# Self attention in steps of one sequence: near and far queries together on TensorE, scores over all 128 rows, one PSUM bank of values

## Chip, cores and metric

One NeuronCore of a Trainium2 chip runs the whole program. The metric is the device time of one execution in microseconds; a program's time is the median of its runs. Lower is better.

## What is computed

A decoder block on x of shape (32, 64, 512): self attention, cross attention to a context of the same shape, and a feed-forward part with routed experts, each with a residual sum. Only the self attention is touched. From the reference, cut down:

```python
q = (x @ wq).reshape(b, s, 32, 16)        # 32 heads of 16, s = 64
k = (x @ wk).reshape(b, s, 8, 16)         # 8 groups, each shared by 4 heads
v = (x @ wv).reshape(b, s, 8, 16)
scores = einsum('bihd,bjhd->bhij', q, repeat(k, 4)) * 16 ** -0.5
scores = where(tril(ones(s, s)), scores, finfo.min)
out = einsum('bhij,bjhd->bihd', softmax(scores), repeat(v, 4))
x = x + out.reshape(b, s, 512) @ wo
```

## The kernel before

The batch is worked in two halves of 16 sequences (8 tiles of 128 tokens, two sequences in each). Each half passes through projections, self attention, cross attention and the feed-forward part. Every engine has a program of its own, written out by hand, and semaphores tie them: a `wait_ge` holds back all that stands behind it on that engine.

`self_attention(half)` works in **units**. Unit u is sequence b = u // 2 with the query rows l = u % 2: the near half (l = 0, queries 0 to 31, which see 32 keys) or the far half (l = 1, queries 32 to 63, which see 64 keys). With 4 heads a group and 32 queries a unit's scores have 128 rows, and 8 groups times 32 or 64 keys as columns: 256 or 512. There are 32 units in a half.

- Keys are spread out for all groups at once: `spread_keys(b)` on DVE (line 1408) multiplies the sequence's transposed keys `kt` by a selector and writes `kbd` (in the space `kspace`), which has two buffers. Before, `gsel4` keeps 4 groups in 64 rows each, so `kbd` has 4 x 64 columns and the scores come from two matmuls of 64 rows.
- Scores: `scores1(u)` on PE writes two half banks (`pair`): two bf16 matmuls with an identity add the causal mask (line 615), two plain 32-bit matmuls over 64 rows each the scores (line 620). It waits for `kbd_done` and for the copy of the unit before.
- Softmax: `copy_scores` (ACT, 1028) takes the scores to `prob`, which has six buffers (`URING`); `unit_max` (DVE, 1417), `unit_subtract_max` (POOL, 1745), `unit_exps` (ACT, 900), `unit_sums` (DVE, a sum at 1422 and a reciprocal at 1425), `unit_normalise` (POOL, 1751).
- `transpose_probs` (PE, 473) transposes into the bank `pt`, `evacuate_probs` (ACT, 904) copies that to `probt`.
- `values1` (PE, 635) makes four matmuls over 32 columns of the array with `vbd`, the values as `spread_values` (ACT, 1022) lays them out. Four units fill one of two banks `ot`; `output_hi` (ACT, 907) and `output_lo` (DVE, 1301 through 1230) split it into two 32-bit parts.
- `project_part` (PE, 484 through 429 to 431) makes a quarter of the output projection of a tile, three matmuls; `updated` (DVE, 1429) adds it to x. Then follow the statistics of the second norm, `second_norm`, its transposition (PE, 447) and its split.
- Work from elsewhere fills the gaps: the self queries 5 to 7 (`self_query_part`, three matmuls each), and the splits of the weights for cross attention (`split_piece`: ACT 887, POOL 1720).

The engines' loops run over u, w and v, one unit at a time. PE computes the scores of unit u + 4 (`LEAD`), transposes u and takes the values of u - 1, then a part of a projection. On DVE the spreading of keys stands ahead of the maximum of the unit that is two ahead of its use:

```python
for w in range(UNITS1 + 4):                      # DVE
    if w % 2 == 0 and 2 <= w // 2 + 1 < NSEQ:
        spread_keys(w // 2 + 1)
    if w < UNITS1:
        unit_max(w)
    if 1 <= w <= UNITS1:
        unit_sums(w - 1)
```

## Time and profile before

| | |
|---|---|
| median of 3 runs | 1687.55 us (1687.44 to 1689.91) |
| the profiled execution | 1689.26 us, span of its profile 1687.5 us |
| busy over the span: PE | 1621.2 us, 96% |
| PE weight loads | 1328.7 us, 79% |
| DVE | 1111.7 us, 66% |
| ACT | 750.4 us, 44% |
| POOL | 622.8 us, 37% |
| the chain that ended last, by engine | PE 88%, DVE 6%, ACT 2%, issue 2% |

PE is TensorE, DVE VectorE, ACT ScalarE, POOL GpSimd. Busy time is the time in which at least one instruction of the engine ran. The chain is followed back from the last instruction, at each step to what released it. Two stretches of the span hold the self attention: about 65 to 160 us for the first half and 898 to 993 us for the second. A plain 32-bit matmul leaves two records, one of a 32-bit transposition one, and records of neighbours overlap, since each counts a pipeline's latency; what an instruction takes in a stream is the distance from start to start.

### The profile page before, as it was taken

Reading aid. Unit: us, or ns where it says so; the run is one execution under the profiler, and the core shown is the slowest. Engines: PE = TensorE matmul, PEld = TensorE weight load, DVE = VectorE, ACT = ScalarE, POOL = GpSimd, SP = SyncE. Lnnn points to the kernel's source line nnn. Section 1 sums busy time; section 2 is a strip of 40 time slices with the busy share of each in tenths; the row PEclk is TensorE's granted clock in tenths of the full one; section 3 lists DMA queues with packets and bytes.
Section 4 is the critical chain, followed back from the end, with each engine's and each line's share of the span. In section 5 each row is a group of like instructions: output and inputs, shape, how many; then the busy total and the mean of one; then the engine's idle time right before and its main releaser. Section 6 shows DMA issues by size and latency. Waiting matters only on the chain.

```text
span 1687.5 us, 41365 instructions
## 1 busy us (share of the span) xinstructions
PE 1621.2 (96%) x17048; PEld 1328.7 (79%) x17048; DVE 1111.7 (66%) x1979; ACT 750.4 (44%) x1396; POOL 622.8 (37%) x515
## 2 busy tenths in 40 slices
PE   5899999999999999999988999999999999998998
PEld 5556788888888888788865578888888888886897
DVE  4477767676766676874544868676676767668643
ACT  2585535354454444431225745455353544443221
POOL 3484423334243332460125834243233342434500
PEclk9999999999999999999999999999999999998999
DMA  4210112021020120121121102021020110201100
GB/s 167 63 45 1 26 40 63 0 62 44 19 62 8 54 68 0 51 82 47 46 61 61 32 1 64 2 63 37 25 62 0 62 44 19 68 18 46 39 20 26
DMA packets 26254, 71.59 MB, mean 42 GB/s; under 512 B 3136, under 2 KB 3392, under 8 KB 26176
## 3 DMA queue, kind: packets, MB, share of 16 engines
q1 hardware_dynamic: 26176, 70.48, 13.5%
q8 instruction: 57, 0.93, 0.2%
q14 instruction: 21, 0.17, 0.0%
HBM read 66.27 MB, written 4.19 MB: 42 GB/s over the span
## 4 chain that ended last, share of the span: by engine, by line
PE 88%; DVE 6%; ACT 2%; issue 2%; POOL 1%; DMA 1%; POOLq 0%; SPq 0%; DVEq 0%; ACTq 0%
PE acc L429 15%; PE acc L430 14%; PE acc L431 13%; PE y L429 10%; PE y L431 9%; PE y L430 9%; PE quad L707 5%; PE quad L736 4%; PE y L720 2%; PE y L473 2%; PE quad L620 2%; PE quad L635 1%; DVE kv L1391 1%; PE acc L447 1%; DVE qb L1395 1%
## 5 line engine op out<-in xcount | busy, mean ns | idle before, releaser
L1724 POOL TENSOR_TENSOR qkrs<-qkve,mhalf 128x10 f32<-128x10 f32 x64 | 125.1, 1954 | 328.9 <-DVE qkve L1383 328.9
L429 PE MATMUL y<-w_hi 128*128 128x512 f32 x576 | 233.6, 405 | 10.8 <-DVE w_lo L1230 9.7
L429 PE MATMUL acc<-w_hi,xn_hi 128*128 128x512 f32 (+1 forms) x576 | 228.0, 396 | 10.5 <-DVE xn_lo L1230 10.5
L430 PE MATMUL y<-w_lo,w_hi 128*128 128x512 f32 x576 | 226.5, 393 | 0.0
L431 PE MATMUL y<-w_hi,w_lo 128*128 128x512 f32 x576 | 226.2, 393 | 0.0
L430 PE MATMUL acc<-w_lo,xn_hi 128*128 128x512 f32 (+1 forms) x576 | 221.6, 385 | 0.0
L431 PE MATMUL acc<-w_hi,xn_lo 128*128 128x512 f32 (+1 forms) x576 | 219.8, 382 | 0.0
L1720 POOL TENSOR_TENSOR w_lo<-stage,w_hi 128x1024 fp32r<-128x1024 f32 (+1 forms) x88 | 171.6, 1958 | 86.1 <-ACT w_hi L887 86.1
L1306 DVE TENSOR_TENSOR x<-y,x 128x512 f32<-128x512 f32 x128 | 88.4, 691 | 146.5 <-PE y L431 146.5
L1377 DVE TENSOR_REDUCE qkss<-kspace 128x4 f32<-128x512 f32 x128 | 87.4, 683 | 110.9 <-ACT kspace L926 110.2
L429 PE MATMUL acc<-w_hi,cx_hi 128*128 128x256 f32 x512 | 151.1, 295 | 1.7 <-DVE xn_lo L1230 1.7
L429 PEld LDWEIGHTS acc<-w_hi,xn_hi 128*128 128x128 f32 x576 | 110.7, 192 | 50.6 <-issue 23.9
L430 PE MATMUL acc<-w_lo,cx_hi 128*128 128x256 f32 x512 | 145.8, 285 | 0.0
L431 PE MATMUL acc<-w_hi,cx_lo 128*128 128x256 f32 x512 | 145.8, 285 | 0.0
L1733 POOL TENSOR_TENSOR prob<-prob,pmax 128x512 f32<-128x512 f32 x64 | 69.3, 1082 | 206.6 <-DVE pmax L1289 206.6
L429 PEld LDWEIGHTS y<-w_hi 128*128 128x128 f32 x576 | 109.1, 189 | 43.3 <-issue 22.8
L1101 ACT COPY probt<-y 128x512 f32<-128x512 f32 x64 | 37.6, 588 | 234.5 <-PE y L720 234.5
L887 ACT CAST w_hi<-stage 128x1024 fp32r<-128x1024 f32 (+1 forms) x116 | 104.8, 918 | 82.0 <-PE y L431 63.9
L431 PEld LDWEIGHTS acc<-w_hi,xn_lo 128*128 128x128 f32 x576 | 110.8, 192 | 21.6
L431 PEld LDWEIGHTS y<-w_hi,w_lo 128*128 128x128 f32 x576 | 109.3, 190 | 23.5
L430 PEld LDWEIGHTS y<-w_lo,w_hi 128*128 128x128 f32 x576 | 109.4, 190 | 20.2
L430 PEld LDWEIGHTS acc<-w_lo,xn_hi 128*128 128x128 f32 x576 | 110.9, 193 | 18.0
(139 smaller groups left out, 3737.4 us busy)
## 6 DMA issues: line engine op xcount, KB each, us to landing
stage<-in_w_cross SPq DMA_DIRECT2D x64, 512.0 KB, 3.7
stage<-in_w_cross SPq DMA_DIRECT2D x32, 256.0 KB, 2.8
stage<-in_w_ffn SPq DMA_DIRECT2D x16, 512.0 KB, 3.6
x<-in_x SPq DMA_DIRECT2D x8, 512.0 KB, 4.0
stage<-in_w_self SPq DMA_DIRECT2D x8, 512.0 KB, 4.8
kt<-in_ctx SPq DMA_DIRECT2D x16, 256.0 KB, 3.0
out_x<-x SPq DMA_DIRECT2D x16, 256.0 KB, 2.0
stage<-in_w_self SPq DMA_DIRECT2D x4, 256.0 KB, 4.5
```

The source lines that it names most:

```text
L429: nc.tensor.matmul(target, l_hi, r_hi, start=first, stop=False)
L430: nc.tensor.matmul(target, l_hi, r_lo, start=False, stop=False)
L431: return nc.tensor.matmul(target, l_lo, r_hi, start=False, stop=last)
L707: ins = nc.tensor.matmul(quad[h * SEQ:(h + 1) * SEQ, i, t * SEQ:(t + 1) * SEQ], q2t[rows, t, j, 2 * h:2 * h + 2, :].rearrange("p h q -> p ...
L736: ins = nc.tensor.matmul(ot[:, b, t * 256:(t + 1) * 256], kv[rows, 2 * (k % CHUNKS) + t, P:2 * P], probs, start=True, stop=True)
L887: nc.scalar.copy(target, stage[:, place.slot(n), 0:width]).then_inc(w_hi_done, 1)
L1101: nc.scalar.copy(probt[:, k % 2, :], y[0][:]).then_inc(pt_done.sem, 1)
L1306: nc.vector.tensor_tensor(x[:, i % NT, :], y[i % 2][:], x[:, i % NT, :], ALU.add).then_inc(y_free.sem, 1)
L1377: nc.vector.tensor_reduce(qkss[:, k % 2, t * REP:(t + 1) * REP], qsq[:, t], AX_X, ALU.add).then_inc(q_sum.sem, 1)
L1720: nc.gpsimd.tensor_tensor(low, stage[:, place.slot(n), 0:width], high.bitcast(F32), ALU.subtract).then_inc(w_lo_done, 1)
L1724: return nc.gpsimd.tensor_tensor(target, source, mhalf[:, 0:width], ALU.pow)
L1733: nc.gpsimd.tensor_tensor(pr, pr, spread(pmax[:, buffer, :], 8, SEQ), ALU.subtract).then_inc(s_sub.sem, 1)
```

## The change

Every loop of the self attention now goes over p, one sequence a step, with both its units. In a step p PE makes the scores of sequence p + 2 (`AHEAD`), the values of both units of p - 1, the transpositions of both units of p, and two parts of a projection.

- `kbd` has 8 groups x 64 keys (512 columns), each group's keys in its own 16 of 128 rows, so the scores of a unit are one matmul over 128 rows. The near unit's has 256 columns, the far one's 512. The mask comes behind them, one matmul of 256 columns each, the far one's over the far 32 keys alone. Each unit's scores have a bank (`sc[0]`, `sc[1]`).
- `gsel4` and its making go; `causal_b` has 8 x 32 columns.
- Transpositions alternate between two banks (`pt`), one of which was a bank of values; the values have one bank, `ot1`, so the first values of a tile wait for `output_lo` of the tile before.
- On DVE `spread_keys(p + 3)` stands behind the maxima and sums of the step and behind `output_lo`.

```diff
-                    pe.wait_ge(s_add.sem, at(s_add, u))
-                    keys = slice(0, SEQ) if l else slice(0, SEQ // 2)
-                    masks = slice(0, SEQ) if l else slice(SEQ // 2, SEQ)
-                    for t in range(2):
-                        nc.tensor.matmul(pair[:, t, :, keys], ident_b[:], causal_b[:, :, masks],
-                                         start=True, stop=False)
-
-                    for t in range(2):
-                        rows = slice(t * SEQ, (t + 1) * SEQ)
-                        ins = nc.tensor.matmul(pair[:, t, :, keys], q1t[rows, b, l].rearrange("p r q -> p (r q)"),
-                                               kbd[rows, b % 2, :, keys], start=False, stop=True)
-                    ins.then_inc(sc_rdy.sem, 1)
+                    near, far = (slice(l * SEQ // 2, (l + 1) * SEQ // 2) for l in range(2))
+                    queries = [q1t[:, b, l].rearrange("p r q -> p (r q)") for l in range(2)]
+
+                    pe.wait_ge(s_add.sem, at(s_add, max(2 * b - 1, 0)))
+                    nc.tensor.matmul(sc[0], queries[0], kbd[:, b % 2, :, near], start=True, stop=False)
+                    pe.wait_ge(s_add.sem, at(s_add, 2 * b))
+                    nc.tensor.matmul(sc[1], queries[1], kbd[:, b % 2], start=True, stop=False)
+                    nc.tensor.matmul(sc[0], ident_b[:], causal_b[:], start=False, stop=True).then_inc(sc_rdy.sem, 1)
+                    nc.tensor.matmul(sc[1][:, :, far], ident_b[:], causal_b[:], start=False, stop=True
+                                     ).then_inc(sc_rdy.sem, 1)
...
                     if u % 4 == 0:
-                        pe.wait_ge(ot_lo_done.sem, at(ot_lo_done, i - 1))
+                        pe.wait_ge(ot_lo_done.sem, at(ot_lo_done, i))
...
+                for p in range(NSEQ + 1):
+                    if p + AHEAD < NSEQ:
+                        scores1(p + AHEAD)
+                    if p == 0:
+                        query_parts(0)
+                    if p >= 1:
+                        values1(2 * p - 2)
+                        values1(2 * p - 1)
+                    if p < NSEQ:
+                        transpose_probs(at, 2 * p, (2 * p) % URING)
+                        transpose_probs(at, 2 * p + 1, (2 * p + 1) % URING)
+                    if 0 < p < 4:
+                        query_parts(p)
+                    if p == 4:
                         pieces_split(place, 5)
-                    if u >= 8:
-
-                        i = (u - 8) // 4
-                        project_part(at, i, i + 1, u % 4, self_y(i), i)
-                    if u >= 16 and u % 4 == 0:
-                        second_norm((u - 16) // 4)
-                for h in range(1, REP):
+                    if p >= 4:
+
+                        i = (p - 4) // 2
+                        for h in (2 * (p % 2), 2 * (p % 2) + 1):
+                            project_part(at, i, i + 1, h, self_y(i), i)
+                    if p >= 8 and p % 2 == 0:
+                        second_norm((p - 8) // 2)
+                for h in (2, 3):
                     project_part(at, 6, 7, h, self_y(6), 6)
...
+                for p in range(-AHEAD, NSEQ + 1):
+                    scored = p + AHEAD < NSEQ
+                    if p == -1:
                         self_queries(half, 5)
...
+                    if scored:
+                        copy_scores(2 * (p + AHEAD))
+                    if 0 <= p + 1 < NSEQ:
+                        unit_exps(at, 2 * (p + 1) + 1)
+                    if scored:
+                        copy_scores(2 * (p + AHEAD) + 1)
+                        unit_exps(at, 2 * (p + AHEAD))
...
+                for p in range(-AHEAD, NSEQ + 1):
+                    scored = p + AHEAD < NSEQ
+                    if p >= 6 and p % 2 == 0:
+                        updated((p - 6) // 2)
+                    if p >= 9 and p % 2 == 1:
+                        second_norm_lo((p - 9) // 2)
+                    if scored:
+                        unit_max(2 * (p + AHEAD))
+                    if 0 <= p + 1 < NSEQ:
+                        unit_sums(2 * (p + 1) + 1)
+                    if scored:
+                        unit_max(2 * (p + AHEAD) + 1)
+                        unit_sums(2 * (p + AHEAD))
+                    if p >= 2 and p % 2 == 0:
+                        output_lo(at, (p - 2) // 2)
+                    if 2 <= p + 3 < NSEQ:
+                        spread_keys(p + 3)
...
+                for p in range(-AHEAD, NSEQ):
+                    scored = p + AHEAD < NSEQ
+                    if scored:
+                        unit_subtract_max(at, 2 * (p + AHEAD))
+                    if p >= 7 and p % 2 == 1:
+                        layernorm_rstd(at, NT, (p - 7) // 2)
+                    if 0 <= p + 1 < NSEQ:
+                        unit_normalise(at, 2 * (p + 1) + 1)
+                    if scored:
+                        unit_subtract_max(at, 2 * (p + AHEAD) + 1)
+                        unit_normalise(at, 2 * (p + AHEAD))
```

The last three loops are those of ACT, DVE and POOL; the order of PE's and DVE's instructions decides most, and so it is shown twice.

First PE, in the steady part of the stage, before the change: one sequence, that is two units. `quad<-causal_b` is the mask, `quad<-kspace,qb` the scores, `y1<-ident,prob` the transpositions, `quad<-probt,vbd` the values.

```order
L615 MATMUL quad<-causal_b,ident_b 128x4x32 [waits s_add,kbd_done]
L615 MATMUL quad<-causal_b,ident_b 128x4x32
L620 MATMUL quad<-kspace,qb 128x4x32 x2
L473 MATMUL y1<-ident,prob 128x128 [waits pt_done,s_nrm]
L473 MATMUL y1<-ident,prob 128x128 x3
L635 MATMUL quad<-probt,vbd 32x4x32 [waits vbd_done,pt_done]
L635 MATMUL quad<-probt,vbd 32x4x32 x3
L429 MATMUL acc1<-xn_hi,w_hi 128x512
L430 MATMUL acc1<-xn_lo,w_hi 128x512
L431 MATMUL acc1<-xn_hi,w_lo 128x512
L615 MATMUL quad<-causal_b,ident_b 128x256 [waits s_add,kbd_done]
L615 MATMUL quad<-causal_b,ident_b 128x256
```

And PE after the change, one step:

```order
L616 MATMUL quad<-kspace,qb 128x256 [waits s_add,kbd_done]
L618 MATMUL quad<-kspace,qb 128x512 [waits s_add]
L619 MATMUL quad<-causal_b,ident_b 128x256
L620 MATMUL quad<-causal_b,ident_b 128x8x32
L634 MATMUL quad<-probt,vbd 32x4x32 [waits vbd_done,pt_done]
L634 MATMUL quad<-probt,vbd 32x4x32 x3
L634 MATMUL quad<-probt,vbd 32x4x32 [waits vbd_done,pt_done]
L634 MATMUL quad<-probt,vbd 32x4x32 x3
L475 MATMUL quad<-ident,prob 128x128 [waits pt_done,s_nrm]
L475 MATMUL quad<-ident,prob 128x128 x3
L475 MATMUL y1<-ident,prob 128x128 [waits pt_done,s_nrm]
L475 MATMUL y1<-ident,prob 128x128 x3
```

The same kinds of matmul stand together, and `kbd_done` is waited for once a sequence, ahead of everything else of the step.

Then DVE, before: two units and the keys of the sequence after. `kspace<-kt,gsel4` is `spread_keys`.

```order
L1408 TENSOR_TENSOR kspace<-kt,gsel4 128x256 [waits sc_rdy]
L1417 TENSOR_REDUCE pmax<-prob 128x8 [waits s_add]
L1422 TENSOR_REDUCE psum_<-prob 128x8 [waits s_exp]
L1425 RECIPROCAL prec<-psum_ 128x8 [waits s_sum]
L1417 TENSOR_REDUCE pmax<-prob 128x8 [waits s_add]
L1422 TENSOR_REDUCE psum_<-prob 128x8 [waits s_exp]
L1425 RECIPROCAL prec<-psum_ 128x8 [waits s_sum]
L1230 TENSOR_TENSOR w_lo<-quad,w_hi 128x2x4x64 [waits ot_hi_done]
L1408 TENSOR_TENSOR kspace<-kt,gsel4 128x256 [waits sc_rdy]
```

And DVE after the change, one step with an `output_lo`:

```order
L1418 TENSOR_REDUCE pmax<-prob 128x8 [waits s_add]
L1423 TENSOR_REDUCE psum_<-prob 128x8 [waits s_exp]
L1426 RECIPROCAL prec<-psum_ 128x8 [waits s_sum]
L1418 TENSOR_REDUCE pmax<-prob 128x8 [waits s_add]
L1423 TENSOR_REDUCE psum_<-prob 128x8 [waits s_exp]
L1426 RECIPROCAL prec<-psum_ 128x8 [waits s_sum]
L1234 TENSOR_TENSOR w_lo<-quad,w_hi 128x2x4x64 [waits ot_hi_done]
L1409 TENSOR_TENSOR kspace<-kt,gsel 128x512 [waits sc_rdy]
```

The four reductions that now stand ahead of `kspace` are the near maximum of sequence p + 2, the far sum of p + 1, the far maximum and the near sum of p + 2; `kspace` is for p + 3. So the keys of sequence b stand behind all of the reductions of the near unit of b - 1; before, they stood ahead of the first one.

## Rows read from the trace of the kernel before

**Rows 1.** Windows: us; busy us of PE, PEld, DVE, ACT, POOL; PE clock, DMA, GB/s
```profile
100.00:130.00 30.00, 30.00 (x252) 17.93 (x251) 25.18 (x58) 23.12 (x52) 26.26 (x29) 1.00 0.15 46
890.00:910.00 20.00, 16.11 (x86) 11.13 (x85) 7.46 (x18) 8.89 (x20) 6.77 (x8) 0.91 0.19 67
```

**Rows 2.** Waits, 64 to 160 us: engine line <- releaser: total us, times, longest us
```profile
PEld quad L615 <- DVE kspace L1408: 0.6, 2, 0.3
```

**Rows 3.** Timeline, PE, one sequence: start, us, what; later [idle before <-releaser]
```profile
101.55 0.29 PE L615 MATMUL quad<-causal_b,ident_b 128*128 128x128 bf16 x2
101.76 0.49 PE L620 MATMUL quad<-kspace,qb 64*128 64x128 f32 x4
102.19 0.66 PE L473 MATMUL y<-ident,prob 128*128 128x128 f32 x4
102.77 0.43 PE L635 MATMUL quad<-probt,vbd 128*32 128x128 f32 x8
...
103.95 0.40 PE L615 MATMUL quad<-causal_b,ident_b 128*128 128x256 bf16 x2
104.27 0.70 PE L620 MATMUL quad<-kspace,qb 64*128 64x256 f32 x4
104.91 0.66 PE L473 MATMUL y<-ident,prob 128*128 128x128 f32 x4
...
106.67 0.29 PE L615 MATMUL quad<-causal_b,ident_b 128*128 128x128 bf16 x2
```

**Rows 4.** Chain of waits: plain 32-bit matmuls, 128 rows, 512 columns (two records each)
```profile
60.48 3.44 PE y L497 x8
```

**Rows 5.** Timeline, PE: scores of sequence 0, 2, 15; first matmul after the stage
```profile
68.17 0.28 PE L615 MATMUL quad<-causal_b,ident_b 128*128 128x128 bf16 x2
...
76.19 0.27 PE L615 MATMUL quad<-causal_b,ident_b 128*128 128x128 bf16 x2 [0.78 <-ACT prob L1028]
...
143.62 0.28 PE L615 MATMUL quad<-causal_b,ident_b 128*128 128x128 bf16 x2
...
160.35 0.28 PE L429 MATMUL acc<-w_hi,cx_hi 128*128 128x256 f32 x1
```

**Rows 6.** Timeline, ACT: copy of near scores, then the exponential of far ones
```profile
92.49 0.37 ACT L1028 COPY prob<-quad 128x256 f32<-128x256 f32 x1 [0.52 <-PE quad L620]
92.76 0.63 ACT L900 ACTIVATE prob<-prob 128x512 f32<-128x512 f32 x1
```

**Rows 7.** Timeline, DVE, the stage of the first half
```profile
85.88 0.69 DVE L1417 TENSOR_REDUCE pmax<-prob 128x8 f32<-128x512 f32 x1 [1.74 <-ACT prob L1028]
86.48 0.41 DVE L1422 TENSOR_REDUCE psum_<-prob 128x8 f32<-128x256 f32 x1
86.93 0.20 DVE L1425 RECIPROCAL prec<-psum_ 128x8 f32<-128x8 f32 x1
87.05 0.92 DVE L1408 TENSOR_TENSOR kspace<-kt,gsel 128x256 f32<-128x256 f32 x1
...
92.00 0.69 DVE L1230 TENSOR_TENSOR w_lo<-quad,w_hi 128x512 fp32r<-128x512 f32 x1
...
93.32 0.41 DVE L1417 TENSOR_REDUCE pmax<-prob 128x8 f32<-128x256 f32 x1
93.65 0.67 DVE L1422 TENSOR_REDUCE psum_<-prob 128x8 f32<-128x512 f32 x1
94.35 0.20 DVE L1425 RECIPROCAL prec<-psum_ 128x8 f32<-128x8 f32 x1
```

**Rows 8.** Timeline, POOL, the same stage
```profile
86.65 1.04 POOL L1745 TENSOR_TENSOR prob<-prob,pmax 128x512 f32<-128x512 f32 x1 [1.39 <-DVE pmax L1417]
...
94.64 1.04 POOL L1751 TENSOR_TENSOR prob<-prob,prec 128x512 f32<-128x512 f32 x1 [0.21 <-DVE prec L1425]
```

**Rows 9.** Timeline, POOL and DVE, two instructions that meet
```profile
77.22 1.31 POOL L1745 TENSOR_TENSOR prob<-prob,pmax 128x512 f32<-128x512 f32 x1
...
77.25 0.37 DVE L1408 TENSOR_TENSOR kspace<-kt,gsel 128x256 f32<-128x256 f32 x1
```

More of the change, by code:

```diff
@@ L39 @@
 ACC3 = NT + 7 * CHUNKS
-LEAD = 4
+AHEAD = 2
 PRING = 4
@@ L641, in self_attention @@
                 scores1(0)
-                self_query_part(half, 5, 0)
-                self_query_part(half, 5, 1)
+                self_queries(half, 5)
                 scores1(1)
-                self_query_part(half, 5, 2)
-                self_query_part(half, 5, 3)
-                scores1(2)
-                self_query_part(half, 6, 0)
-                scores1(3)
                 def second_norm(i):
@@ L1026, in copy_scores @@
                     act.wait_ge(sc_rdy.sem, at(sc_rdy, u + 1))
-                    target = seen(u, u % URING).rearrange("p (t g) k -> p t g k", t=2)
-                    nc.scalar.copy(target, pair[:, :, :, 0:target.shape[-1]]).then_inc(s_add.sem, 1)
+                    nc.scalar.copy(seen(u, u % URING), sc[u % 2]).then_inc(s_add.sem, 1)
                 spread_values(0)
@@ L1042, in second_norm_hi @@
                     transposed_hi(n_at, n, tile_of(xn_hi, i), ln_hi_done)
-                for w in range(UNITS1 + 4):
-                    if w < UNITS1:
-                        copy_scores(w)
-                    if w == 1:
+                for p in range(-AHEAD, NSEQ + 1):
+                    scored = p + AHEAD < NSEQ
+                    if p == -1:
                         self_queries(half, 5)
-                    if 1 <= w <= UNITS1:
-                        unit_exps(at, w - 1)
-                    if LEAD <= w < UNITS1 + LEAD:
-                        evacuate_probs(at, w - LEAD, (w - LEAD) % 2)
-                    if w in (6, 10):
-                        self_queries(half, w // 4 + 5)
-                    if w >= 9 and w % 4 == 1:
-                        i = (w - 9) // 4
+                    if scored:
[6 more added lines that the diff above has]
+                    if p >= 2 and p % 2 == 0:
+                        i = (p - 2) // 2
@@ L1068, in self_attention @@
+                    if p in (1, 3):
+                        self_queries(half, 6 + p // 2)
+                    if p >= 8 and p % 2 == 0:
+                        second_norm_hi((p - 8) // 2)
+                    if 0 <= p < NSEQ - 2:
+                        spread_values(p + 2)
+                    if p in (2, 4, 6, 8):
+                        act.wait_ge(acc_rdy.sem, at(acc_rdy, A1[half]["q7" if p > 4 else "kv3"] + 1))
+                        split_piece(Place(2, half, 0), (p - 2) // 2)
                 first = Place(2, half, 0)
-                act.wait_ge(pv_done.sem, at(pv_done, UNITS1))
@@ L1811, in self_attention @@
                                  0.0).then_inc(gaps_clear.sem, 1)
-                for v in range(UNITS1 + 1):
-                    if v < UNITS1:
-                        unit_subtract_max(at, v)
-                    if v >= 1:
-                        unit_normalise(at, v - 1)
-                    if v in (7, 11, 15, 19):
-                        split_piece(Place(2, half, 0), (v - 7) // 4)
-                    if v >= 17 and v % 4 == 1:
-                        layernorm_rstd(at, NT, (v - 17) // 4)
-                for i in (4, 5, 6):
+                for p in range(-AHEAD, NSEQ):
+                    scored = p + AHEAD < NSEQ
+                    if scored:
+                        unit_subtract_max(at, 2 * (p + AHEAD))
+                    if p >= 7 and p % 2 == 1:
+                        layernorm_rstd(at, NT, (p - 7) // 2)
[4 more added lines that the diff above has]
+                        unit_normalise(at, 2 * (p + AHEAD))
+                    if p in (2, 4, 6, 8):
+                        split_piece(Place(2, half, 0), (p - 2) // 2)
+                for i in (5, 6):
                     layernorm_rstd(at, NT, i)
```

90 lines of the change are left out of this document (30 added, 60 removed).

## The prediction

> **What bounds the kernel now.** I looked first at the windows, for who is busy in the stage that changes. In its steady part TensorE (PE) is busy for all of the 30 us, POOL for 26.26, DVE for 25.18, and PE's clock is granted in full [rows 1]. So PE sets the pace there, but DVE and POOL have under a sixth of slack, and less than that once an order forces them to wait. Then the waits: in the whole stage of the first half PE waited for the spread keys for 0.6 us, twice, 0.3 us at the longest [rows 2]. Third PE's timeline, for what a sequence costs: from the near unit's mask to that of the next sequence 5.12 us (101.55 to 106.67) [rows 3]. Last the timelines of ACT, DVE and POOL, for the distances from start to start from which a chain can be laid [rows 6 to 8]. I take faster or slower by over 0.2%, 3.4 us, as what a measurement can tell.
>
> **PE's own work.** Before, a sequence's masks and scores take 0.21 + 0.43 for the near unit and 0.32 + 0.64 for the far one, 1.60 us [rows 3]. The 64-row matmul with twice the columns takes only 0.21 more. A plain 32-bit matmul of 512 columns over 128 rows leaves 8 records in 3.44 us for four matmuls, 0.86 each [rows 4], so 128 columns are 0.21: two matmuls of 64 rows therefore run side by side, and the rest of 0.43 and of 0.64, 0.21 both times, is the change from one kind of matmul to the next. After, the near scores take 0.43, the far 0.86, the masks (2 x 256 columns, at 0.11 for the 2 x 128 of before, the part of 0.21 that is no change) 0.21, with a change or two of 0.1 between: 1.6 to 1.7. The scores gain nothing: three changes of kind are saved, and the side-by-side running is lost.
> The Trainium skill has a rule that speaks against this part ("TensorEngine Tiling (Array Packing)", Performance Considerations): a contraction of 64 rows can be packed in two tiles for up to twice the rate, while its Key Properties say that a change of tiling mode drains the engine. By the first alone the scores would cost 0.64 more a sequence; the rows have both.
> The values with a projection part take 1.18 a unit (102.77 to 103.95) and a unit's transpositions 0.58 (102.19 to 102.77) [rows 3]. In pairs I take 2.1 and 1.1, since each change of kind comes once instead of twice (0.1 to 0.15 each, by what is over in the row above). PE's step is then 1.65 + 2.1 + 1.1 = 4.85 against 5.12, a gain of 0.27, if nothing is late: 32 sequences, 8.6 us, at most.
>
> **What is late: the keys.** `scores1(p + 3)` waits for `spread_keys(p + 3)`, and DVE now comes to that only behind the near sum of sequence p + 2, which needs that sequence's scores. So each step closes a loop: scores, softmax of the near unit, keys, scores. I lay it out from the start of a step's scores, S = 0.
> - PE: the near mask, the third matmul, starts at 0.43 + 0.86 + 0.1 = 1.38 and its record is over 0.29 later, at 1.67 (that length is the 0.29 of the two small masks, taken long) [rows 3]. I give ACT 0.05 to see it, by estimate.
> - ACT: copy of the near scores at 1.72, 0.37 long, to 2.09. The far exponential of the sequence before stands behind it and starts 0.27 after its start, at 1.99, to 2.62 [rows 6].
> - DVE: near maximum from about 2.12, 0.41 long; then the far sum, which waits for that exponential: 2.65. From its start to its reciprocal 0.70, at 3.35 (93.65 to 94.35) [rows 7]; next instruction 0.12 later (86.93 to 87.05), the far maximum at 3.47; the near sum 0.60 after it (85.88 to 86.48), 4.07; its reciprocal 0.45 later, 4.52; and 0.12 later, at 4.64, `spread_keys`, or in every second step `output_lo` (0.69, of which 0.09 overlaps), with `spread_keys` at 5.25.
> - The spreading has 512 columns instead of 256. With nothing beside it 256 take 0.37 [rows 9]; 256 more add 0.28, as 0.69 against 0.41 of the reductions shows [rows 7]: 0.65.
> - It meets POOL. In the row at 87.05 it took 0.92: POOL's instruction from 86.65 ended at 87.69 [rows 8], and 0.28 later the keys were done, 87.97. So the two exclude each other, for a whole instruction, and a caught spreading ends 0.28 + 0.28 after POOL's. Here POOL's far normalising starts 0.09 after the far reciprocal's end (94.55 to 94.64) [rows 7, 8], at 3.64, to 4.68; the far subtraction follows at once, to 5.72.
> - Steps without `output_lo`: DVE asks at 4.64, gets its turn at 4.68, is done at 5.24. With PE's start, 0.15 by estimate, the next scores begin at S = 5.4. Steps with it: DVE asks at 5.25, in the far subtraction, waits until 5.72, is done at 6.28; S = 6.4.
> Both are longer than PE's 4.85, so PE waits 0.5 and 1.5 us a step. ACT has 3 copies and 2 exponentials of 0.4 to 0.6 a step besides the copies of probabilities, and ends before its next copy; the norms' work on DVE (about 1.7 in a step) fits into the 2.1 us in which it waits for scores. Those cost nothing. The single bank of values doesn't either: `output_lo` is over ahead of the keys, so ahead of the next scores.
>
> **The sum.** Scores of sequence 0 start at 68.17 as before [rows 5]. Then 1.65, and self query 5 in one piece, 2.8 by estimate (12 matmuls at the 0.23 or so that is left of 1.18 with the values taken out): the scores of sequence 1 at 72.6. Fourteen intervals follow to sequence 15, of which six have an `output_lo`: 8 x 5.4 + 6 x 6.4 = 81.6, so 154.2 in place of 143.62 [rows 5]: 10.6 late. Behind it nothing closes the loop. Before, 16.7 us were left to the first matmul after the stage (160.35); after, the scores (1.65), four pairs of values (2.4) and three of transpositions (3.3), five pairs of projection parts (7.2) and two norm transpositions (0.9, by estimate as the transpositions) come to 15.5, and 0.4 for a wait for `x`: 15.9, 0.8 less. That is 9.8 us a half, 20 in both. The first interval has PE idle for about 3.8 us, and once a stretch with shorter gaps lowered the granted clock to 0.91 on a mean of 20 us [rows 1], which is 3 to 4 us at 1.2 GHz, half the columns a us: I add 1 us a half. Sum: +22 on the profiled execution's 1689.26 us, 1711.3. The median of the runs is 1.7 lower, so I say **1710 us**, against 1687.55.
>
> **Rivals.**
> - *POOL wins each meeting* (0.22). DVE's 4.64 and POOL's 4.68 are close enough to go either way. If the far subtraction gets in first, the steps without `output_lo` are 6.4 too: 8 us more a half, 1726. For it: 0.1 us more on DVE does it. Against: where POOL's record started 0.03 ahead of DVE's, at 77.22, it was POOL that was drawn out, to 1.31 from 1.04, and the keys took their bare 0.37 [rows 9]. The Trainium skill ("SBUF — State Buffer", SBUF: two separate sides) says that whichever of the two starts first keeps the port pair for the whole instruction; by its letter POOL would have it there and often here, which is this rival. The row has the lock, but not by the recorded starts. Between the two lie mixed cases, and the weights' splits (POOL, four steps a half) shift the meeting.
> - *The keys are hardly late* (0.13). If the far sum were ready earlier or hand-overs were shorter, the loop would lose up to 0.4 a step: 5.1 and 6.0, so 5 us a half less, 1700.
> - *It is faster* (0.06). The mechanism: the loop fits beside PE's other work of a step, which is the 3.2 us between two scores. It decides where the near unit's softmax and the spreading take under 3.2 us from the end of the scores; I have 3.75 and 4.75. Then PE's saved changes of kind are paid out: 0.27 a sequence at best, 1680 to 1684. For it only that the 0.6 us of [rows 2] show keys ready before they are wanted, but in the old order.
> - *PE's clock falls throughout* (0.05). With 10 to 20% of idle time in each step the granted clock could drop again and again, as in the second window of [rows 1], where PE was busy for 16.1 of 20 us. At 0.9 over twice 90 us that is some 10 us of PE time more, partly inside the loop: 1720 or more.
>
> **How the numbers follow.** The forecast case has 0.52, with 1704 to 1717 as its own range (0.1 us on each hand-over of the loop makes 3 us in both halves). With the first two rivals it makes 0.87. The range 1698 to 1727 reaches just past both. Slower 0.92, the sum of all cases but one; faster 0.06; the same 0.02, for a loop that is just about as long as PE's step. That the change doesn't do what it says is no case: the order of both engines shows it.
>
> **What would show it.** Right: scores of a sequence 5.3 to 6.5 us apart, shorter and longer in turn; PE's greatest new wait before the scores, for DVE's `kspace`, some 13 to 17 us a half, all of it in that place; `kspace` at 128x512 taking 0.6 to 1.1 us; masks and scores about 1.65 us; sequence 15 near 154. Wrong: no wait for `kspace`; a PE step under 5 us; a wait for values or transpositions in its place; a granted clock well under 1 over the stage.

## The result, and the profile after

| | before | after |
|---|---|---|
| median | 1687.49 us (1686.67 to 1689.91, 4 runs) | 1710.62 us (1707.66 to 1712.84, 4 runs) |
| span of the profiled execution | 1687.5 us | 1709.1 us |
| scores of sequence 0 to the first matmul behind the stage, first half | 92.18 us | 103.11 us |
| the same, second half | 92.18 us | 103.11 us |

The ratio is 1.0128, with a 95% interval of 1.0111 to 1.0146: slower by 23 us. Both halves' stages are 10.93 us longer, 21.9 together, and the spans differ by 21.6: all of the loss lies in the stage that was changed.

The page of after, its first and fourth part (busy time by engine; the chain that ended last):

```profile
PE 1615.4 (95%) x16856; PEld 1337.8 (78%) x16856; DVE 1117.2 (65%) x1977; ACT 750.3 (44%) x1396; POOL 632.6 (37%) x515
...
PE 84%; DVE 10%; ACT 3%; issue 2%; POOL 1%; DMA 1%; POOLq 0%; SPq 0%; DVEq 0%; ACTq 0%
```

PE has 5.8 us less to do than before and the program is 22 us longer. The chain tells why: DVE's share of it rose from 6 to 10%, ACT's from 2 to 3%, and PE's fell from 88 to 84%.

Windows of after, columns as in [rows 1]: the second row is the one that answers to the first of [rows 1], and the first is discussed further down.

```profile
78.90:85.70 6.80, 6.75 (x21) 4.40 (x21) 2.95 (x7) 2.27 (x5) 3.72 (x5) 0.58 0.00 1
100.00:130.00 30.00, 24.79 (x189) 16.55 (x188) 21.02 (x46) 20.31 (x48) 23.19 (x24) 1.00 0.17 53
```

PE is busy for 24.79 of 30 us where it was for 30.00, and each of DVE, ACT and POOL does less in the window too. No engine is full, so what to look for is a loop through several engines.

Waits of after, 64 to 172 us, columns as in [rows 2]:

```profile
DVE pmax L1418 <- ACT prob L1030: 27.1, 16, 4.9
ACT prob L1030 <- PE quad L619: 26.9, 16, 4.8
...
PE quad L616 <- DVE kspace L1409: 16.4, 13, 3.5
```

Read from below, this is the loop: PE's scores wait for DVE's keys (16.4 us, where PE's only wait for them before was that of its weight loads in [rows 2], 0.6), ACT's copies for PE's scores, DVE's maxima for ACT's copies. Then PE's timeline, the starts of the scores of sequences 2 to 5, with most of step 2 from 90.95 on:

```profile
78.91 1.22 PE L616 MATMUL quad<-kspace,qb 128*128 128x256 f32 x2 [3.51 <-DVE kspace L1409]
...
85.67 0.70 PE L616 MATMUL quad<-kspace,qb 128*128 128x256 f32 x2
...
90.95 0.70 PE L616 MATMUL quad<-kspace,qb 128*128 128x256 f32 x2 [0.52 <-DVE kspace L1409]
91.49 1.02 PE L618 MATMUL quad<-kspace,qb 128*128 128x512 f32 x2
92.35 0.27 PE L619 MATMUL quad<-causal_b,ident_b 128*128 128x256 bf16 x1
...
92.66 0.64 PE L634 MATMUL quad<-probt,vbd 128*32 128x128 f32 x16
93.24 0.66 PE L475 MATMUL quad<-ident,prob 128*128 128x128 f32 x4
93.73 0.60 PE L475 MATMUL y<-ident,prob 128*128 128x128 f32 x4
94.08 0.48 PE L429 MATMUL acc<-xn_hi,w_hi 128*128 128x512 f32 x1
...
97.37 0.70 PE L616 MATMUL quad<-kspace,qb 128*128 128x256 f32 x2 [1.65 <-DVE kspace L1409]
```

Scores start 5.28 us apart (85.67 to 90.95) and then 6.42 (to 97.37); the next ones come 5.29 later, at 102.66, and 6.42 after that. Now DVE's timeline of a step with `output_lo`, and the end of the next one without; its scores begin at 90.95 and 97.37.

```profile
93.06 0.42 DVE L1418 TENSOR_REDUCE pmax<-prob 128x8 f32<-128x256 f32 x1 [2.16 <-ACT prob L1030]
...
95.68 0.64 DVE L1234 TENSOR_TENSOR w_lo<-quad,w_hi 128x512 fp32r<-128x512 f32 x1
96.23 1.08 DVE L1409 TENSOR_TENSOR kspace<-kt,gsel 128x512 f32<-128x512 f32 x1
...
101.97 0.64 DVE L1409 TENSOR_TENSOR kspace<-kt,gsel 128x512 f32<-128x512 f32 x1
```

And the POOL instructions that these two spreadings meet:

```profile
95.73 1.04 POOL L1748 TENSOR_TENSOR prob<-prob,pmax 128x512 f32<-128x512 f32 x1
...
102.02 1.49 POOL L1748 TENSOR_TENSOR prob<-prob,pmax 128x512 f32<-128x512 f32 x1
```

In the long step the far subtraction was under way, until 96.77; the keys were done 0.54 later, at 97.31, and PE started 0.06 after that. In the short step DVE asked at 4.60 us from the scores' start, 0.05 ahead of POOL: the keys took their bare 0.64, and POOL's instruction was drawn out to 1.49.

### The profile page after: what moved, and what is told of

Same layout as the page of the kernel before. It is cut to its first block, busy times and chain, and to the rows that moved or that the text cites. A ratio compares the mean times of both kernels' runs of the same rounds, so it can differ in the third digit from the quotient of the medians.

```text
span 1709.1 us, 40947 instructions
## 1 busy us (share of the span) xinstructions
PE 1615.4 (95%) x16856; PEld 1337.8 (78%) x16856; DVE 1117.2 (65%) x1977; ACT 750.3 (44%) x1396; POOL 632.6 (37%) x515
## 3 DMA queue, kind: packets, MB, share of 16 engines
HBM read 66.27 MB, written 4.19 MB: 41 GB/s over the span
## 4 chain that ended last, share of the span: by engine, by line
PE 84%; DVE 10%; ACT 3%; issue 2%; POOL 1%; DMA 1%; POOLq 0%; SPq 0%; DVEq 0%; ACTq 0%
PE acc L429 14%; PE acc L430 13%; PE acc L431 13%; PE y L429 9%; PE y L431 9%; PE y L430 9%; PE quad L710 5%; PE quad L739 4%; PE y L723 2%; PE quad L618 2%; DVE psum_ L1423 1%; PE quad L616 1%; DVE kspace L1409 1%; DVE kv L1393 1%; PE acc L447 1%
## 5 line engine op out<-in xcount | busy, mean ns | idle before, releaser
L890 ACT CAST w_hi<-stage 128x1024 fp32r<-128x1024 f32 (+1 forms) x116 | 104.8, 917 | 81.6 <-PE y L431 64.0
L431 PEld LDWEIGHTS acc<-w_hi,xn_lo 128*128 128x128 f32 x576 | 111.6, 194 | 21.6
```

The lines of the kernel that those rows point to most:

```text
L431: return nc.tensor.matmul(target, l_lo, r_hi, start=False, stop=last)
L890: nc.scalar.copy(target, stage[:, place.slot(n), 0:width]).then_inc(w_hi_done, 1)
```

## The experiments

Three questions were open. Is it the place of the keys behind the near sum, and nothing else, that costs the time? How much of it is POOL? And what would the rest of the change be worth with the keys in time? All ratios are to the kernel before, run beside each. That kernel's median was 1689.17 us beside the first four experiments, 1688.16 beside the next four and 1688.71 beside the last two, against 1687.49 beside the change, so a difference of microseconds between experiments of different groups is known to 1 or 2 us only.

### Keys first in the step

```diff
@@ DVE
                 for p in range(-AHEAD, NSEQ + 1):
                     scored = p + AHEAD < NSEQ
+                    if 2 <= p + 3 < NSEQ:
+                        spread_keys(p + 3)
...
                         output_lo(at, (p - 2) // 2)
-                    if 2 <= p + 3 < NSEQ:
-                        spread_keys(p + 3)
```

> The change with the spreading of keys moved to the head of DVE's step; nothing else. Theory (the keys close a loop behind the near unit's softmax): the wait of TensorE for the spread keys goes, the scores of a sequence start every 4.6 to 4.9 us, set by TensorE's own work of a step (4.6 us from one score to the end of the projection parts in the profile after), and the time falls below the kernel before, 1670 to 1682 us. Rival (the change costs by its wider matmuls and one bank of values, the wait for keys only hides that): TensorE waits in another place instead, for values or transpositions, and the time stays at 1700 us or more.

Measured: 1682.77 us (1680.22 to 1683.5), ratio 0.9958 (0.9942 to 0.9975). That is 28 us under after, by moving two lines, and just above what I expected. PE has no wait for the keys; of its waits for other engines in the first half's stage, 6.0 us in all against 2.3 in the kernel before, the two greatest are:

```profile
PE y L429 <- DVE x L1430: 3.0, 5, 1.1
PE quad L634 <- ACT probt L907: 1.3, 2, 0.7
```

One step of PE's timeline shows what the change itself does to PE, where nothing is late (from 95.08, behind a step of the same kinds):

```profile
95.08 0.59 PE L616 MATMUL quad<-kspace,qb 128*128 128x256 f32 x2
95.50 1.02 PE L618 MATMUL quad<-kspace,qb 128*128 128x512 f32 x2
96.36 0.27 PE L619 MATMUL quad<-causal_b,ident_b 128*128 128x256 bf16 x1
96.47 0.27 PE L620 MATMUL quad<-causal_b,ident_b 128*128 128x256 bf16 x1
96.67 0.64 PE L634 MATMUL quad<-probt,vbd 128*32 128x128 f32 x16
...
99.58 0.59 PE L616 MATMUL quad<-kspace,qb 128*128 128x256 f32 x2
```

The step is 4.50 long, against 5.12 in [rows 3]: 0.62 a sequence, 20 us for 32. Only 6 arrive. The steps on both sides of this one are 4.87 and 4.92 long, since the values wait for `vbd` (0.30 and 0.35 us, ACT's spreading of the values). Two steps of the half are much longer, 7.20 (114.00 to 121.20) and 7.25 (125.71 to 132.96). POOL, DVE and PE in the first of them:

```profile
112.35 2.39 POOL L1723 TENSOR_TENSOR w_lo<-stage,w_hi 128x1024 fp32r<-128x1024 f32 x1 [0.60 <-ACT w_hi L890]
...
115.79 0.42 DVE L1423 TENSOR_REDUCE psum_<-prob 128x8 f32<-128x256 f32 x1 [1.20 <-ACT prob L903]
...
117.03 1.53 DVE L1409 TENSOR_TENSOR kspace<-kt,gsel 128x512 f32<-128x512 f32 x1
...
119.31 0.47 PE L429 MATMUL y<-w_hi 128*128 128x512 f32 x1 [1.08 <-DVE x L1430]
```

POOL's split of a weight, 2.39 us, holds back the near subtraction, behind it the near exponential and `probt` (PE waits 0.62 us for that at 116.28), and the near sum, for which DVE stands idle 1.20 us. Then the keys take 1.53 us beside POOL's far subtraction, and `updated` (`x`) stands behind them. In this late part of the stage, where `updated` and the second norm's work are added, DVE has no slack to catch up:

```profile
130.00:145.00 15.00, 13.69 (x108) 9.60 (x108) 14.64 (x36) 11.42 (x29) 11.60 (x14) 1.00 0.01 2
```

A full DVE is still not the pace of each step: within this window one step takes 4.51 (132.96 to 137.47). `kspace` takes 1.00 us on the mean in this run against 0.87 in after, both in the first half's stage: here more of it falls on POOL's instructions.

### Keys ahead of `output_lo`

```diff
+                    if 2 <= p + 3 < NSEQ:
+                        spread_keys(p + 3)
                     if p >= 2 and p % 2 == 0:
                         output_lo(at, (p - 2) // 2)
-                    if 2 <= p + 3 < NSEQ:
-                        spread_keys(p + 3)
```

> The spreading one place earlier, ahead of output_lo and behind the near sum. Theory: the six longer intervals of a half (6.4 us) become as short as the others (5.3), 13 us less than the change in both halves, 1697 us. Rival (the long intervals come from other work that falls into each second step, the update of x or the weights' splits): no change, 1710 us.

Measured: 1702.89 us (1700.88 to 1703.68), ratio 1.0078 (1.0062 to 1.0095), 7.7 under after. In the early part the long interval is gone:

```profile
84.84 0.70 PE L616 MATMUL quad<-kspace,qb 128*128 128x256 f32 x2 [1.26 <-DVE kspace L1409]
90.13 0.70 PE L616 MATMUL quad<-kspace,qb 128*128 128x256 f32 x2 [0.53 <-DVE kspace L1409]
95.55 0.70 PE L616 MATMUL quad<-kspace,qb 128*128 128x256 f32 x2 [0.65 <-DVE kspace L1409]
```

They are 5.29 and 5.42 apart, and so on. So the 6.42 of every second step in after is `output_lo` and the POOL instruction that its delay runs into. Later two steps go wrong again, 6.45 us (117.14 to 123.59) and 7.04 (129.01 to 136.05). The step behind the second, 6.89, is another matter: its granted clock is 0.66 from 135 to 140 us, and the same step of the second half takes 5.42. DVE and POOL ahead of the first of the two:

```profile
118.52 2.37 POOL L1723 TENSOR_TENSOR w_lo<-stage,w_hi 128x1024 fp32r<-128x1024 f32 x1
...
120.86 0.61 POOL L1748 TENSOR_TENSOR prob<-prob,pmax 128x256 f32<-128x256 f32 x1
...
121.95 0.42 DVE L1423 TENSOR_REDUCE psum_<-prob 128x8 f32<-128x256 f32 x1 [0.70 <-ACT prob L903]
...
122.52 1.01 DVE L1409 TENSOR_TENSOR kspace<-kt,gsel 128x512 f32<-128x512 f32 x1
```

POOL's split of a weight, 2.37 us, holds back the near subtraction, with it the exponential, the near sum and the keys behind it, which then meet POOL as well. I had expected 1697 us, some 6 us too low; the late steps of both halves, 6.45 and 7.04 against the 5.3 or so that I took, make up 5.8 of that. It is again the near sum ahead of the keys, by another road.

### Keys ahead of the near sum

```diff
                     if scored:
                         unit_max(2 * (p + AHEAD) + 1)
+                    if 2 <= p + 3 < NSEQ:
+                        spread_keys(p + 3)
+                    if scored:
                         unit_sums(2 * (p + AHEAD))
```

and the two lines at the end of the step go.

> The spreading one place earlier again, between the far maximum and the near sum, so DVE asks for it some 0.57 us sooner than in the run before. Theory with the lock (a tensor operation of DVE with two SBUF inputs and one of POOL exclude each other for a whole instruction): POOL is in the far normalising then, the keys are done at its end and no sooner than in the run before, intervals stay at 5.2 to 5.4 us, 1695 to 1698 us. Rival without a lock (POOL only slows DVE in proportion, or not at all): the intervals fall by the 0.57 us to 4.7 or so, 1682 us.

Measured: 1694.87 us (1694.16 to 1697.82), ratio 1.0039 (1.0025 to 1.0053), just under what I expected. DVE comes to the keys 0.57 us earlier than in the run before this one (a near sum and a reciprocal), and yet the early intervals are the same: 5.28 (76.74 to 82.02), 5.29, 5.42, 5.28. DVE and POOL of this run:

```profile
85.67 1.04 POOL L1755 TENSOR_TENSOR prob<-prob,prec 128x512 f32<-128x512 f32 x1 [0.42 <-DVE prec L1426]
86.06 1.20 DVE L1409 TENSOR_TENSOR kspace<-kt,gsel 128x512 f32<-128x512 f32 x1
86.67 1.49 POOL L1749 TENSOR_TENSOR prob<-prob,pmax 128x512 f32<-128x512 f32 x1
```

The keys begin while POOL normalises the far unit, which ends at 86.71, and are done at 87.26, 0.55 behind it. So what was won in the order was lost to the exclusion of the two engines. POOL's instruction starts at a fixed distance from the far reciprocal, so any place of the keys between the two should end the same (not tried). Of the gain over the run before, 8 us, the two stages give 4.5 in the profiled executions (3.0 and 1.5), from their late part, where the near sum no longer holds the keys; the rest lies outside them and was not traced.

### Keys ahead of the far maximum

```diff
                     if 0 <= p + 1 < NSEQ:
                         unit_sums(2 * (p + 1) + 1)
+                    if 2 <= p + 3 < NSEQ:
+                        spread_keys(p + 3)
                     if scored:
                         unit_max(2 * (p + AHEAD) + 1)
```

> The spreading between the far sum and the far maximum. Theory with the lock: DVE asks at about 3.5 us of the step, ahead of POOL's far normalising, so the keys are done at about 4.1 us and TensorE's own 4.6 us set the interval again: 1675 to 1684 us, close to the run with the keys first. If the lock theory is wrong, this run lies a further 0.7 us a step below the one with the keys ahead of the near sum, or equals it at TensorE's bound.

Measured: 1681.88 us (1680.31 to 1683.75), ratio 0.9959 (0.9945 to 0.9973): as with the keys first. Early intervals are 4.5 to 4.6; PE still waits 4.2 us for the keys in the stage, five times. One reduction of 0.55 us from its start to the next one's, between this place and the last, is worth 13 us, because the keys now slip in ahead of POOL's normalising.

### The order of before, scores over 128 rows

The prediction gave nothing for this part. To see it alone, the kernel before gets the wide keys and the matmuls of the change, unit by unit:

```diff
-        kbd = kspace[:, 0:512].rearrange("p (r g k) -> p r g k", r=2, g=4)
+        kbd = kspace[:].rearrange("p (r g k) -> p r g k", r=2, g=NG)
...
-                    for t in range(2):
-                        nc.tensor.matmul(pair[:, t, :, keys], ident_b[:], causal_b[:, :, masks],
-                                         start=True, stop=False)
...
+                    nc.tensor.matmul(sc[l], q1t[:, b, l].rearrange("p r q -> p (r q)"), kbd[:, b % 2, :, keys],
+                                     start=True, stop=False)
+                    nc.tensor.matmul(sc[l][:, :, last], ident_b[:], causal_b[:], start=False, stop=True
+                                     ).then_inc(sc_rdy.sem, 1)
```

> The kernel before with one part of the change alone: keys in 8 groups, a unit's scores one matmul over 128 rows with the mask behind it; order, steps and the banks of values as before. Theory (two 64-row matmuls ran side by side, 128 rows lose that and save some changes of kind): a sequence's masks and scores take 1.9 us against 1.60, 0.33 more by the distances in the profile after (0.54 and 0.21 for the near unit, 0.11, 0.86 and 0.21 for the far one), 32 sequences, 8 to 12 us slower than before, 1696 to 1700 us. Rival (the scores are neutral, as the 1.7 us in the new step suggest): within 3 us of before. Rival (two matmuls fewer are a gain): faster.

Measured: 1682.23 us (1680.78 to 1683.87), ratio 0.9965 (0.9953 to 0.9978). I expected it slower, and it is 6 us faster. PE's timeline, a far and a near unit:

```profile
98.52 1.02 PE L613 MATMUL quad<-kspace,qb 128*128 128x512 f32 x2
99.38 0.27 PE L615 MATMUL quad<-causal_b,ident_b 128*128 128x256 bf16 x1
99.48 0.60 PE L472 MATMUL y<-ident,prob 128*128 128x128 f32 x4
...
101.17 0.59 PE L613 MATMUL quad<-kspace,qb 128*128 128x256 f32 x2
101.61 0.27 PE L615 MATMUL quad<-causal_b,ident_b 128*128 128x256 bf16 x1
101.71 0.60 PE L472 MATMUL y<-ident,prob 128*128 128x128 f32 x4
```

Far scores and mask take 0.96, near ones 0.54: 1.50 against the 1.60 of [rows 3]. The transpositions that begin at 101.71 last until the values at 102.24: 0.53 against 0.58. From plain 32-bit matmul to bf16 mask and on to the transposition nothing is lost: the far scores take 0.86, as in [rows 4], and the mask 0.10, as between the two masks of the run with the keys first (96.36 to 96.47). I had charged such changes 0.1 each. What costs is a change of the array's shape. In [rows 3] the visit to 64 rows costs 0.3 us a unit: 0.10 at the masks (0.21 and 0.32 for a bare 0.11 and 0.21) and 0.21 at the scores. That is 0.64 a sequence, and the side-by-side running saves 0.54 of the bare 1.50. The order of before has room for the wider keys on DVE (12.38 of 15 us busy from 130 on, 13.26 here). In the profiled executions, whose spans are 7.5 us apart, the two stages give only 3.0. Another 3.5, by an estimate from the granted clock, lie behind them: it is granted at 0.93 from 160 to 185 us and at 0.94 from 990 to 1020 us before, and at 1.00 in both stretches here, with PE busy for the same time. So some 3 us are shown for the scores. Whether the change brings about the clock was not tried.

### Keys first, and masks and scores over 64 rows

If packing costs only by its changes of shape, then in the grouped order, where it has one change in and one out a sequence, it should win: half the columns on PE, and half on DVE for the keys.

```diff
+                    for t in range(2):
+                        nc.tensor.matmul(quad[:, t, 0:384], ident_b[:], causal_b[:], start=True, stop=False)
+                    for t in range(2):
+                        ins = nc.tensor.matmul(sc[0][:, t], queries[t][0], kbd[halves[t], b % 2, :, near],
+                                               start=False, stop=False)
+                    for t in range(2):
+                        ins = nc.tensor.matmul(sc[1][:, t], queries[t][1], kbd[halves[t], b % 2],
+                                               start=False, stop=True)
+                    ins.then_inc(sc_rdy.sem, 2)
```

in place of the four matmuls; `kbd` has 4 groups again, and the keys stand first.

> The first run of this study (keys at the head of DVE's step) with the scores back in two matmuls of 64 rows a unit, behind one mask of 384 columns a bank; keys in 4 groups, 256 columns. Theory: grouping by kind is the gain and the 128 rows a loss inside it. Masks and scores take 0.32 + 0.64 + 0.2 to 0.3, 1.2 us, against 1.67, so 0.45 us a sequence while TensorE sets the pace, less where DVE does: 6 to 14 us below that run, 1668 to 1676 us. Rival (DVE is already full at 4.5 us a step): no more than 3 us below it.

Measured: 1675.21 us (1674.56 to 1675.56), ratio 0.9921 (0.9905 to 0.9938), 7.6 under keys first over 128 rows. DVE is still busy for 14.61 of 15 us from 130 to 145, and PE's greatest waits are for `probt` (2.4 us) and for `x` (2.3 us, four times).

### The same, keys ahead of the far maximum

The diff is that of the experiment of this name above, on the kernel just shown.

> The same 64-row scores with the keys between the far sum and the far maximum, where the 128-row version started its scores 4.5 us apart. Theory: 1668 to 1676 us as well; the update of x no longer stands behind the keys, so the waits for x go, and it is within 3 us of the run before it. Rival: the loop over the keys binds again as TensorE's step falls to 4.1 us, intervals of 4.2 to 4.6 us, 1672 to 1680 us.

Measured: 1674.77 us (1673.62 to 1675.47), ratio 0.9918 (0.9901 to 0.9934). No difference in time between the two places: the waits for `x` (0.3) are exchanged for waits for the keys (3.7, three times) and for `output_lo`:

```profile
PE quad L640 <- DVE w_lo L1240: 1.6, 4, 0.4
```

That is the single bank of values, up to 0.4 us at a time once nothing else is late. The clock adds to it: in the first half the step from 77.28 to 83.92 took 6.64 us, at a granted clock of 0.50 (78 to 83), where it takes 5.21 in the second half. The first half's stage is 1.45 us longer than in the run before it, the second's 0.57 shorter.

### The changed kernel, masks and scores over 64 rows

Scores as in the last two, the keys where the change has them, behind `output_lo`.

> The changed kernel as it is, keys in its place behind output_lo, with the 64-row scores and keys of 256 columns. Theory (the loop is scores, near softmax, keys): near scores are handed over some 0.4 us sooner and the keys take 0.28 less, so the short intervals fall from 5.3 to about 4.65 us; the long ones, which end with POOL's far subtraction, by the same: 15 to 20 us below the change, 1691 to 1696 us. Rival (the interval is set by DVE's and POOL's work, not by a loop through the scores): less than 5 us below the change.

Measured: 1695.47 us (1691.49 to 1696.49), ratio 1.0044 (1.0029 to 1.0058), 15 under after and within what was expected. Its intervals are 4.72 and 5.85 (93.07 to 97.79 to 103.64). The loop is the same, with its parts on PE and DVE shortened. A PE step, from 93.07:

```profile
93.07 0.50 PE L620 MATMUL quad<-causal_b,ident_b 128*128 128x384 bf16 x2 [1.50 <-DVE kspace L1420]
93.50 0.49 PE L622 MATMUL quad<-kspace,qb 64*128 64x128 f32 x4
93.82 0.60 PE L625 MATMUL quad<-kspace,qb 64*128 64x256 f32 x4
94.35 0.64 PE L640 MATMUL quad<-probt,vbd 128*32 128x128 f32 x16
```

Masks and scores take 1.28 (93.07 to 94.35) against 1.71 in after (90.95 to 92.66), both behind a wait.

### The same, keys one sequence further ahead

The rival to the loop was that the place costs time by what DVE or POOL do there. This kernel leaves the place, the load and the matmuls of the run above (called f4 in the text below) and removes only the dependence: four buffers, and the keys for p + 4.

```diff
-                    if b >= 2:
-                        dve.wait_ge(sc_rdy.sem, at(sc_rdy, 2 * b - 2))
-                    nc.vector.tensor_tensor(kbd[:, b % 2], kt[:, b * SEQ:(b + 1) * SEQ].unsqueeze(1).to_broadcast(
+                    if b >= 4:
+                        dve.wait_ge(sc_rdy.sem, at(sc_rdy, 2 * b - 6))
+                    nc.vector.tensor_tensor(kbd[:, b % 4], kt[:, b * SEQ:(b + 1) * SEQ].unsqueeze(1).to_broadcast(
...
-                    if 2 <= p + 3 < NSEQ:
-                        spread_keys(p + 3)
+                    if 2 <= p + 4 < NSEQ:
+                        spread_keys(p + 4)
```

> The changed kernel with 64-row scores and the keys in the place that the change gave them, behind output_lo, but spread for the sequence after the next one (p + 4 in place of p + 3), with four key buffers of 256 columns in place of two. The amount of work and its place on DVE are those of f4; only the dependence is one step longer. Theory (the loss is the dependence, not the place or the load): the wait of TensorE for kspace goes but for the first steps, and the time is that of the keys at the head of the step, 1670 to 1678 us. Rival (a late place costs by itself, or DVE's load binds): 1688 us or more, near f4's 1695.

Measured: 1676.15 us (1675.94 to 1676.85), ratio 0.9929 (0.9911 to 0.9948), 19 us under the run above. PE never waits for the keys; its step is 4.19 long where nothing is late (94.06 to 98.25). `kspace` itself takes 0.73 us on the mean here, more than the 0.62 of the run above: its meetings with POOL are no rarer. PE does not wait for them. The loss was the dependence, not the place. This is shown with the 64-row scores; with 512 columns of keys four buffers were not tried.

### `updated` first, then the keys, 64 rows

With the keys first and 64-row scores (f2 in the text below) four waits for `x` were left, since `updated` stood behind the keys. The two are exchanged at the head of the step:

```diff
                     if p >= 6 and p % 2 == 0:
                         updated((p - 6) // 2)
+                    if 2 <= p + 3 < NSEQ:
+                        spread_keys(p + 3)
```

> f2 with the update of x ahead of the keys at the head of DVE's step. In f2 TensorE waited for the update of x four times in a half, 2.3 us, since the keys ahead of it wait for POOL. Theory: that wait is put at 0 to 1 us, and the time falls by 1 to 4 us to 1671 to 1674 us, unless DVE's own load, 14.6 of 15 us from 130 to 145 us, holds it: then it stays within 1 us of f2's 1675.

Measured: 1670.68 us (1668.13 to 1672.97), ratio 0.9901 (0.9876 to 0.9925). It beats both kernels, before by 1.0%, and is just under what I expected. Its four runs are 1668.1, 1668.9, 1672.5 and 1673.0, the lower two at a mean granted clock of 0.992 and 0.993, the others at 0.989, so a part of the 4.5 us below the run with the keys first can be the clock; its two stages are 3.6 us shorter. The wait for `x` is down to 0.3 us, and DVE has some slack:

```profile
130.00:145.00 15.00, 14.45 (x142) 10.49 (x132) 13.55 (x36) 12.15 (x31) 11.77 (x16) 1.00 0.01 2
```

## Why the prediction was right

The time (1710 forecast, 1710.62 measured) came out by its mechanism, with two terms mis-sized on the way that the loop hid.

- **The loop.** Right, nearly instruction by instruction. From the scores' start, forecast against the timelines: copy at 1.72, measured 1.71; near maximum 2.12, 2.11; the keys in a short step asked for at 4.64, 4.60, done at 5.24, 5.24; in a long step 5.25, 5.28, done at 6.28, 6.36. Intervals 5.4 and 6.4 were 5.3 and 6.4: PE starts 0.05 behind the keys, not 0.15. Three fell outside the 5.3 to 6.5 or out of turn: 5.19, the first (73.72 to 78.91), 6.76, the second, and 6.03, a later short one (132.81 to 138.84). Sequence 15 stood at 157.01, not 154.2: 1.3 of that is that this stage began at 69.45 and not at 68.17.
- **POOL.** In the long steps POOL had it and in the short ones DVE had it, as forecast, but by 0.05 us. The likeliest rival stood as close as that. The Trainium skill's rule ("SBUF — State Buffer", SBUF: two separate sides), that whichever starts first keeps the ports, agrees with the short step (keys 101.97, POOL 102.02) and with the long one (POOL 95.73, keys 96.23), and not with [rows 9], where POOL's record starts first and DVE has its way.
- **The sum.** From the scores of sequence 1 to those of 15: forecast 81.6, measured 83.3 (73.72 to 157.01). Of the 1.7 over, 1.5 is the interval 78.91 to 85.67: 6.76 where the same one in the run with the keys ahead of `output_lo` took 5.29 (79.55 to 84.84). Its window shows a granted clock of 0.58, so most of it at 1.2 GHz, after PE had waited for 3.51 us. The second half has the same 6.76. I had 1 us a half for this. The tail behind sequence 15 was 15.55 against 15.9. A half's stage was forecast 10.8 longer and is 10.9 longer.
- **The waits.** 13 to 17 us a half for `kspace`, and 16.4 measured; no other new wait over 1.5 us on PE.
- **PE's own step: wrong, 4.85 forecast.** It is 4.50. The term that failed is "In pairs I take 2.1 and 1.1": values and projections do take 2.06 (0.58 and 1.48 in the run with the keys first, 96.67 to 97.25 and 98.10 to 99.58), but the transpositions 0.85. That is 0.106 each for eight. By it four take 0.42, and the other 0.16 of the 0.58 in [rows 3] is change of array shape: 0.05 in from 64 rows, which is gone where no unit has them (0.53), and 0.11 out to the values' 32 columns, which the pairs don't pay since a projection follows. I had taken 0.58 as nearly all the matmuls' own.
- **"The scores gain nothing" came out by two errors that cancel.** With nothing late they take 1.59 against 1.60. But each change between kinds over 128 rows was charged 0.1 and costs nothing, and the change to the values' 32 columns, 0.1, was left out here. Unit by unit, without that change, they gain 0.1 a sequence.
- **The rival "it is faster".** It turned on the keys being in time and put a value on it of 1680 to 1684. The run with the keys first gave 1682.77, but by another sum: PE's step gains 0.62 and not 0.27, and the waits for `x`, `probt` and `vbd` (3.7 us a half more than before) take over half of it back. So the bound held by luck.
- **Costs put at nothing.** ACT and the norms' work cost nothing here, right. The single bank neither, in after; it costs up to 0.4 us at a time when the keys are early.

**Why the change lost:** with nothing late its grouping of PE's work saves 0.62 us a sequence, up to 20 us. One place in DVE's order cost 28 us (1710.62 against 1682.77 with the keys first), and of the 20, 6 are left once that is mended. The keys of sequence b were made behind reductions that need the scores of b - 1, so no two sequences could overlap beyond that.

## What to carry to other kernels

When work is regrouped into longer steps, write down for each prefetch what stands ahead of it in its engine's order and whether any of that needs the previous step of the engine it feeds. If so, the distance in the program ("for p + 3") is an illusion: if the loop is longer than the step of the busiest engine it sets the pace, and no engine looks full. Move such an instruction ahead of the dependent ones or give it a buffer more, and then look for the engine that becomes full next.

## What was unexpected of the hardware

- TensorE went from plain 32-bit matmul to bf16 and to 32-bit transposition without any loss, as long as all used 128 rows and 128 columns of the array (0.86 and 0.10 us from start to start). From the transpositions on to the projection it isn't free: the first matmul there takes 0.32 us and the next 0.22 (98.10, 98.42, 98.64 in the run with the keys first). Changes of shape cost: about 0.3 us for a visit to 64 rows, and about 0.2 for one to 32 columns, 0.11 on the way in and 0.12 on the way out (four matmuls there take 0.35 in the kernel before, 110.60 to 110.95, and eight 0.58, so four are bare 0.23). So packing two contractions of 64 rows lost against one of 128 when done unit by unit (1.60 against 1.50) and won when grouped (1.28 against 1.71, both behind a wait; 1.29 against 1.59 with nothing late, 94.06 to 95.35 and 95.08 to 96.67).
- I had looked for the exclusion of DVE and POOL in DVE's spreading only. In the run with the keys ahead of `output_lo` the normalising `xn<-x`, one tensor with a mean and a factor per row, took 1.26 us beside a POOL instruction that was itself drawn out to 1.49; in the kernel before it takes 0.52 on the mean of the first half's stage.

```profile
122.95 1.49 POOL L1748 TENSOR_TENSOR prob<-prob,pmax 128x512 f32<-128x512 f32 x1
123.46 1.26 DVE L1441 TENSOR_SCALAR xn<-x,mv,rstd 128x512 f32<-128x512 f32 x1
```

- In after a wait of 3.51 us on PE was followed by some 5 us at mostly half the clock (0.55 in the window 80 to 85) in the first half, and in the second by the same step of 6.76 us. In the run with the keys ahead of `output_lo` the same wait was followed by a step of 5.29 at full clock in the first half and by one of 6.76 in the second (918.55 to 925.31). What decides between the two was not tried.
